# One more product of the identity ahead of the waits of o, h2 and yT in a two-layer transformer block kernel

## The chip, the cores and the metric

The kernel runs on one core of one Trainium2 chip. Times are microseconds on the device of one launch, from few repeated runs of the same program; the profiled execution is a run of its own.

## The reference

Sixteen sequences of 128 tokens with 128 features pass through two layers, each with self-attention, cross-attention to a context of 120 tokens, and an MLP:

```python
# layer 0, of x (16, 128, 128), context (16, 120, 128), condition c (16, 128); 16 heads of 8
shift_a, scale_a, gate_a, shift_m, scale_m, gate_m = split(silu(c) @ W_mod + b_mod, 6)
x = x + gate_a * (attention(modulate(ln(x), shift_a, scale_a)) @ W_proj + b_proj)
x = x + (cross_attention(ln(x), ln(context)) @ W_cproj + b_cproj)
h = gelu(modulate(ln(x), shift_m, scale_m) @ W_mlp1 + b_mlp1)
x = x + gate_m * (h @ W_mlp2 + b_mlp2)
# layer 1: the same three units with rotary positions, norms modulated by the condition, and no gates
x = x + attention(adaln(x)) @ sa_out_w.T
x = x + cross_attention(adaln(x), context) @ ca_out_w.T
x = x + (gelu(adaln(x) @ ffn_w1.T + ffn_b1) @ ffn_w2.T + ffn_b2)
```

## The kernel before, in words

The sixteen sequences are four streams of four (CB = 4, 512 columns). An attention unit f is one stream in one of four attention stages a (self and cross of layer 0, self and cross of layer 1), so there are 16 of them; the MLP units m are eight. Units are cut into steps, and make_plan() sorts all steps by times written out by hand in the table T. TensorE, SyncE and GpSimd go through the plan in that order, VectorE and ScalarE in the order of a second key (late). The order does not depend on what is ready: every engine works its list in turn, and semaphores hold it at a step whose data or buffer is missing.

The spine of the plan is the attention: a step "score" (L956) makes the scores of four heads into ps_sc, ScalarE takes their exponentials in two ACTIVATEs (L844), and "value" (L973) multiplies them with the values. The next score waits until both exponentials of the one before are done. All the rest stands between scores: norm transposes (xT, L879), projections (L918, L925), products for the row maxima (L936) with VectorE's reductions (L684) and their transpose (L942), transposes of the normalised sums (L982), the attention's output and the MLP.

Apart from ps_sc and ps_ao, all products go into five PSUM banks in turn (ps_misc, BANKS = 5). fill(n) waits until the reader of the use five before has finished. Then the step waits for its data. The steps that the change touches, all on TensorE:

- o (L992), only in the first self-attention stage, which has a gate: four times. It waits for attT, which ScalarE writes (L855). VectorE multiplies the result with the gate (yT_sb, L715).
- h2 (L1005), the second MLP product of layer 0: four times, four matmuls each. It waits for the four GELUs of ScalarE (hT, L861), which follow the four products of the first matrix (L999).
- yT (L1026), four transposes of yT_sb; behind o and behind h2, so eight times. It waits for VectorE's yT_sb; VectorE then adds the result to x (L728), whose statistics (L579, L582) and the root on GpSimd (L748) lead to the next normalised xn (L589).
- xT (L879), four transposes of xn, 24 times. It has two products ahead of its wait (warm, L875): the identity with the 384 columns of the constants, into the bank that the transposes then overwrite. Their result is read by nobody.

The other units end in a step "out" (L1019), which has no yT.

Of the kernel before, what the change touches and what calls it, by code (L numbers as in the profile page):

```python
# [61 lines left out]
PAIR = 2 * VW  # L62
VSLOTS = 3
PSLOTS = 4
WARM = 2


WCOLS = {}
# [27 lines left out]
NCONST = 3 * P  # L96
# [18 lines left out]
class Step:  # L115
# [34 lines left out]
    xT=(-32.06, -29.2, -31.0, -33.04),  # L150
# [184 lines left out]
def block_kernel(nc, weights, biases, consts, x_in, ctx_in, ctxT_in, rows_in, q_mem, k_mem, m_mem, out):  # L335
    plan, late, uses = make_plan()

    with ExitStack() as ctx:
# [88 lines left out]
        def bank(n):  # L427
            return ps_misc[:, n % BANKS, :]
# [62 lines left out]
        with nc.Block() as block:  # L491
# [374 lines left out]
            def _(pe):  # L866
                def fill(n):

                    if n >= BANKS:
                        pe.wait_ge(S[uses[n - BANKS][0]], uses[n - BANKS][1])  # L870

                def warm(use):

                    for _ in range(WARM):
                        pe.matmul(bank(use)[:, 0:NCONST], ident, cst[:, :], start=True, stop=True)  # L875

                def turn(src, use, rows=P):
                    for b in range(CB):
# [11 lines left out]
                for st in plan:  # L890
                    if st.kind == "xT":
                        fill(st.use)
                        warm(st.use)
                        pe.wait_ge(S["xn_ready"], CB * (st.k + 1))
                        turn(xn, st.use)
                    elif st.kind == "cT":
# [31 lines left out]
                    elif st.kind == "max":  # L928
                        ns = ns_of(st)
                        if st.b == 0:  # L930
                            pe.wait_ge(S["kd_ready"], HG * (st.f + 1))
                            pe.wait_ge(S["q_high"], st.f + 1)
                        for n in range(NG):
                            rows = slice(ROWS * n, ROWS * n + ROWS)
                            fill(st.use + n)
                            pe.matmul(bank(st.use + n)[:, 0:HG * ns], Qh[rows, st.f % 2, st.b * P:(st.b + 1) * P],  # L936
                                      Kd[rows, st.f % 2, :, st.b * ns:(st.b + 1) * ns],
                                      start=True, stop=True).then_inc(S["misc_filled"], 1)
                    elif st.kind == "mT":
                        fill(st.use)  # L940
                        pe.wait_ge(S["max_taken"], GROUPS * (st.f + 1))
                        pe.transpose(bank(st.use)[0:CB * H, 0:P], maxima[:, :, :].rearrange("p h b -> p (h b)"),  # L942
                                     ident).then_inc(S["misc_filled"], 1)
                    elif st.kind == "score":
                        ns = ns_of(st)
                        if st.b == 0 and st.g == 0:
                            pe.wait_ge(S[f"keys_in{st.f % 2}"], 16 * HG * (st.f // 2 + 1))
                            pe.wait_ge(S[f"queries_in{st.f % 2}"], 16 * HG * (st.f // 2 + 1))
                            pe.wait_ge(S[f"maxima_in{st.f % 2}"], 16 * HG * (st.f // 2 + 1))
                        if st.k:  # L950
                            pe.wait_ge(S["probs_ready"], GP * st.k)
                        for i in range(GP):
                            n = GP * st.g + i
                            for side in range(GP):
                                rows = slice(2 * TROWS * side, 2 * TROWS * side + TROWS + SR + 1)
                                ins = pe.matmul(ps_sc[0:ns, side, i * E * P:(i + 1) * E * P],  # L956
                                                Ks[rows, st.f % 2, n, st.b * ns:(st.b + 1) * ns],
                                                Qd[rows, st.f % 2, n, :, st.b * P:(st.b + 1) * P],
                                                start=True, stop=True)
                                if i == GP - 1:  # L960
                                    ins.then_inc(S[f"scores_ready{side}"], 1)
                    elif st.kind == "value":
                        ns = ns_of(st)
                        pe.wait_ge(S["probs_ready"], GP * (st.k + 1))
                        if st.b == 0 and st.g == 0:
                            pe.wait_ge(S["v_ready"], st.f + 1)
                        if st.k % CB == 0 and st.k:
                            pe.wait_ge(S["sums_copied"], st.k // CB)
                        heads = V[0:ns, st.f % VSLOTS, st.b, :, :].rearrange("p h r -> p (h r)")
                        for odd in range(2):  # L970
                            for c in range(HG):
                                at = PAIR * (HG * (GP * st.g + odd) + c) - VW * odd
                                last = pe.matmul(ps_ao[32 * c:32 * c + PAIR, st.b * P:(st.b + 1) * P],  # L973
                                                 heads[:, at:at + PAIR],
                                                 PT[0:ns, st.k % PSLOTS, c // E, odd, c % E, :],
                                                 start=not odd, stop=bool(odd))
                        last.then_inc(S["values_done"], 1)
                    elif st.kind == "norm":
                        fill(st.use)
                        pe.wait_ge(S["sums_copied"], st.k + 1)  # L980
                        for b in range(CB):
                            last = pe.transpose(bank(st.use)[:, b * P:(b + 1) * P],  # L982
                                                AOs[:, st.k % 2, b * P:(b + 1) * P], ident)
                        last.then_inc(S["misc_filled"], 1)
                    elif st.kind == "aT":
                        fill(st.use)
                        pe.wait_ge(S["att_ready"], CB * (st.f + 1))
                        turn(att, st.use)
                    elif st.kind == "o":
                        fill(st.use)  # L990
                        pe.wait_ge(S["attT_ready"], st.f + 1)
                        pe.matmul(bank(st.use), w(f"o{st.a}"), attT[:, :], start=True,  # L992
                                  stop=True).then_inc(S["misc_filled"], 1)
                    elif st.kind == "h":
                        fill(st.use)
                        pe.wait_ge(S["xnT_ready"], CB * (feeds["mlp", st.m] + 1))
                        if st.k == 0:
                            pe.wait_ge(S["rest_in"], 16)
                        pe.matmul(bank(st.use), w(f"w1_{st.a}", st.j), xnT[:, feeds["mlp", st.m] % 2, :],  # L999
                                  start=True, stop=True).then_inc(S["misc_filled"], 1)  # L1000
                    elif st.kind == "h2":
                        fill(st.use)
                        pe.wait_ge(S["hT_ready"], FF * (st.m + 1))
                        for j in range(FF):
                            last = pe.matmul(bank(st.use), w(f"w2_{st.a}", j), hT[:, j, :], start=(j == 0),  # L1005
                                             stop=(j == FF - 1))
                        last.then_inc(S["misc_filled"], 1)
                    elif st.kind == "out":

                        fill(st.use)  # L1010
                        if st.m is None:
                            pe.wait_ge(S["attT_ready"], st.f + 1)
                            parts = [(attT[:, :], w(f"o{st.a}"))]
                        else:
                            pe.wait_ge(S["hT_ready"], FF * (st.m + 1))
                            parts = [(hT[:, j, :], w(f"w2_{st.a}", j)) for j in range(FF)]
                        for b in range(CB):
                            for i, (src, weight) in enumerate(parts):
                                last = pe.matmul(bank(st.use)[:, b * D:(b + 1) * D], src[:, b * P:(b + 1) * P],  # L1019
                                                 weight, start=(i == 0), stop=(i == len(parts) - 1))  # L1020
                        last.then_inc(S["misc_filled"], 1)
                    elif st.kind == "yT":
                        fill(st.use)
                        pe.wait_ge(S["y_ready"], st.k + 1)
                        for b in range(CB):
                            last = pe.transpose(bank(st.use)[:, b * P:(b + 1) * P], yT_sb[:, b * P:(b + 1) * P],  # L1026
                                                ident)
                        last.then_inc(S["misc_filled"], 1)
# [71 lines left out]
```

## Time and profile before

| | us |
|---|---|
| median of 3 runs | 487.15 |
| lowest and highest | 484.03, 489.1 |
| profiled execution | 482.83 |
| its span, first to last instruction | 481.0 |
| mean granted TensorE clock of that span | 0.950 of full speed |

A row of the timeline is a group of instructions of one line that follow each other: its start in us from the span's start, its length, engine, line, operation and operands, how many, and in brackets how long the engine had been idle before it and who ended that. A float32 matmul that is no transpose shows two records. A row of the chain shows its start, its share on the chain and whose it is.

### The profile page before, as it was taken

The page shows a single profiled execution, that of the slowest core. Times are in us where ns is not written, and L with a number is a line of the kernel's source. Part 1 is how long each engine was busy: PE and PEld are TensorE (multiplying, and loading weights), DVE is VectorE, ACT ScalarE, POOL GpSimd, SP SyncE. Part 2 cuts the span into 40 slices and gives each one's busy share as a digit, 9 for nine tenths or more (in the row PEclk, how much of TensorE's full clock was granted, in tenths as well). Part 3 has the DMA queues.
Part 4 walks back from the last instruction along what each step waited for, and adds up shares of the span by engine and source line. Part 5 has one row for each costly group of instructions (what it writes and reads, how often), then busy time and mean ns, then how long its engine had stood idle before and what let it go on. Part 6 is the DMA issues. An engine that isn't in the chain of part 4 may idle for free.

```text
span 481.0 us, 10127 instructions
## 1 busy us (share of the span) xinstructions
PE 402.3 (84%) x3840; PEld 247.6 (51%) x3840; DVE 329.8 (69%) x841; ACT 267.8 (56%) x503; POOL 158.9 (33%) x138
## 2 busy tenths in 40 slices
PE   1855778899889979879888978989899998989696
PEld 1522444565565544544544534555565664747464
DVE  2666567899898963982974946878898994731331
ACT  1111265657666656465476556556565667576552
POOL 5762351651735520250241321335160542020130
PEclk9965699999999999998999989989999998999899
DMA  8860728285845631611613522545557472330001
GB/s 255 287 197 0 216 59 244 51 248 144 239 136 139 198 69 68 128 71 67 133 69 100 104 94 79 131 136 142 155 135 175 150 182 94 86 70 23 3 0 46
DMA packets 31272, 59.22 MB, mean 123 GB/s; under 512 B 3455, under 2 KB 7807, under 8 KB 30975
## 3 DMA queue, kind: packets, MB, share of 16 engines
q1 hardware_dynamic: 30935, 58.35, 44.1%
q8 instruction: 31, 0.51, 0.4%
q10 hardware_dynamic: 288, 0.21, 0.1%
q14 instruction: 18, 0.15, 0.1%
HBM read 31.81 MB, written 26.74 MB: 122 GB/s over the span
## 4 chain that ended last, share of the span: by engine, by line
PE 53%; DVE 16%; ACT 12%; POOL 10%; issue 5%; DMA 2%; SPq 1%; ACTq 0%; DVEq 0%; POOLq 0%
PE ps_ao L973 9%; POOL Kd L764 8%; PE ps_misc L999 7%; PE ps_sc L956 7%; DVE maxima L684 6%; PE ps_misc L875 6%; ACT PT L844 6%; PE ps_misc L918 5%; PE ps_misc L1019 4%; PE ps_misc L936 4%; PE ps_misc L879 4%; ACT xnT L830 3%; DVE xn L589 3%; PE ps_misc L1005 3%; POOL rstd L748 2%
## 5 line engine op out<-in xcount | busy, mean ns | idle before, releaser
L844 ACT ACTIVATE PT<-ps_sc 128x512 f32<-128x512 f32 (+1 forms) x256 | 138.9, 596 | 78.2 <-PE ps_sc L956 77.4
L684 DVE TENSOR_REDUCE maxima<-ps_misc 128x4 f32<-128x512 f32 (+1 forms) x256 | 154.1, 665 | 38.1 <-PE ps_misc L936 37.9
L764 POOL TENSOR_SCALAR Kd<-Kh,head_rows 128x512 fp32r<-128x512 f32 (+1 forms) x64 | 98.5, 1556 | 111.9 <-ACT Kh L804 82.4
L956 PE MATMUL ps_sc<-Qd,Ks 57*128 57x256 f32 (+1 forms) x512 | 64.6, 330 | 17.2 <-ACT PT L844 14.2
L973 PE MATMUL ps_ao<-PT,V 120*18 120x128 f32 (+1 forms) x2048 | 70.6, 277 | 2.8 <-ACT PT L844 2.7
L745 POOL TENSOR_SCALAR vareps<-mv 128x4 f32<-128x4 f32 (+1 forms) x28 | 6.8, 242 | 189.1 <-DVE mv L582 188.6
L956 PEld LDWEIGHTS ps_sc<-Qd,Ks 57*128 57x128 f32 (+1 forms) x512 | 37.7, 183 | 52.7 <-ACT PT L844 27.8
L830 ACT ACTIVATE xnT<-ps_misc,vec 128x128 f32<-128x128 f32 x80 | 30.1, 456 | 56.3 <-PE ps_misc L879 44.6
L973 PEld LDWEIGHTS ps_ao<-PT,V 120*18 120x18 f32 (+1 forms) x2048 | 50.3, 98 | 19.5 <-issue 8.1
L936 PE MATMUL ps_misc<-Kd,Qh 32*128 32x512 f32 (+1 forms) x256 | 42.2, 512 | 10.6 <-POOL Kd L764 8.8
L589 DVE TENSOR_SCALAR xn<-x,mv,rstd 128x128 f32<-128x128 f32 x96 | 36.5, 522 | 11.6 <-POOL rstd L748 11.6
L918 PE MATMUL ps_misc<-xnT,W 128*128 128x512 f32 x72 | 38.7, 653 | 6.8 <-ACT xnT L830 6.3
L875 PE MATMUL ps_misc<-cst 128*128 128x384 f32 x96 | 41.6, 562 | 1.5 <-DVE att L698 1.5
L728 DVE TENSOR_TENSOR x<-ps_misc,x 128x512 f32<-128x512 f32 x24 | 16.5, 687 | 36.9 <-PE ps_misc L1019 33.6
L999 PE MATMUL ps_misc<-xnT,W 128*128 128x512 f32 x64 | 34.3, 686 | 5.7 <-ACT xnT L830 5.0
L936 PEld LDWEIGHTS ps_misc<-Kd,Qh 32*128 32x128 f32 x256 | 17.5, 191 | 27.9 <-POOL Kd L764 9.3
L748 POOL TENSOR_TENSOR rstd<-vareps,minus_half 128x4 f32<-128x4 f32 (+1 forms) x28 | 29.3, 1047 | 2.3
L861 ACT ACTIVATE hT<-ps_misc,bias 128x512 f32<-128x512 f32 x32 | 21.7, 687 | 10.4 <-PE ps_misc L999 9.9
L715 DVE TENSOR_SCALAR yT_sb<-ps_misc,bias,vec 128x128 f32<-128x128 f32 x32 | 10.9, 403 | 23.3 <-PE ps_misc L1005 23.3
L875 PEld LDWEIGHTS ps_misc<-cst 128*128 128x128 f32 x96 | 18.5, 213 | 12.4 <-issue 3.3
L999 PEld LDWEIGHTS ps_misc<-xnT,W 128*128 128x128 f32 x64 | 13.3, 218 | 22.0 <-issue 15.9
L982 PE MATMUL ps_misc<-cst,AOs 128*128 128x128 f32 x128 | 20.2, 280 | 4.3 <-ACT AOs L850 3.3
(77 smaller groups left out, 471.2 us busy)
## 6 DMA issues: line engine op xcount, KB each, us to landing
Qd<-q_mem SPq DMA_DIRECT2D x64, 192.0 KB
k_mem<-Kh SPq DMA_DIRECT2D x16, 512.0 KB, 3.4
q_mem<-Qh SPq DMA_DIRECT2D x16, 512.0 KB, 2.9
Ks<-k_mem SPq DMA_DIRECT2D x32, 192.0 KB
Ks<-k_mem SPq DMA_DIRECT2D x32, 180.0 KB
k_mem<-Kl SPq DMA_DIRECT2D x16, 256.0 KB, 4.0
q_mem<-Ql SPq DMA_DIRECT2D x16, 256.0 KB, 3.0
W<-weights SPq DMA_DIRECT2D x1, 1792.0 KB, 18.5
```

The costliest lines, as they stand in the source:

```text
L589: dve.tensor_scalar(dst[0:rows, b, :], src[0:rows, b, :], mv[0:rows, which, b, 0:1], rstd[0:rows, which, b:b + 1], ALU.subtract, ALU.mult) ...
L684: dve.tensor_reduce(maxima[:, HG * n:HG * n + HG, st.b], bank(st.use + n)[:, 0:HG * ns].rearrange("p (h k) -> p h k", h=HG), AX_X, ALU.max ...
L748: pool.tensor_tensor(rstd[0:rows, which, :], vareps[0:rows, which, :], minus_half[0:rows, :], ALU.pow).then_inc(S["rstd_ready"], 1)
L764: pool.tensor_scalar(Kd[:, st.f % 2, c, 0:n], f32(Kh[:, st.f % 2, 0:n]), head_rows[:, c:c + 1], None, ALU.mult).then_inc(S["kd_ready"], 1)
L830: act.activation(dst[:, b * P:(b + 1) * P], src[:, b * P:(b + 1) * P], ACT.Identity, scale=vec[:, c, m:m + 1], bias=vec[:, c, sh:sh + 1]). ...
L844: act.activation(PT[0:ns, st.k % PSLOTS, g, :, :, :].rearrange("p i e t -> p (i e t)"), ps_sc[0:ns, g, :], ACT.Exp, scale=SCALE).then_inc( ...
L875: pe.matmul(bank(use)[:, 0:NCONST], ident, cst[:, :], start=True, stop=True)
L918: pe.matmul(bank(st.use + i)[:, 0:n], w(f"{st.kind}{st.a}{form}"), src[:, 0:n], start=True, stop=True).then_inc(S["misc_filled"], 1)
L936: pe.matmul(bank(st.use + n)[:, 0:HG * ns], Qh[rows, st.f % 2, st.b * P:(st.b + 1) * P], Kd[rows, st.f % 2, :, st.b * ns:(st.b + 1) * ns], ...
L956: ins = pe.matmul(ps_sc[0:ns, side, i * E * P:(i + 1) * E * P], Ks[rows, st.f % 2, n, st.b * ns:(st.b + 1) * ns], Qd[rows, st.f % 2, n, :, ...
L973: last = pe.matmul(ps_ao[32 * c:32 * c + PAIR, st.b * P:(st.b + 1) * P], heads[:, at:at + PAIR], PT[0:ns, st.k % PSLOTS, c // E, odd, c % ...
L999: pe.matmul(bank(st.use), w(f"w1_{st.a}", st.j), xnT[:, feeds["mlp", st.m] % 2, :], start=True, stop=True).then_inc(S["misc_filled"], 1)
```

## The change

The constant WARM becomes a table by kind of step. xT keeps its two products; o, h2 and yT have one each, placed between the wait for the bank and the wait for the data, into the bank that the step then writes.

```diff
-WARM = 2
+WARM = {"xT": 2, "o": 1, "h2": 1, "yT": 1}
...
-                def warm(use):
-
-                    for _ in range(WARM):
-                        pe.matmul(bank(use)[:, 0:NCONST], ident, cst[:, :], start=True, stop=True)
+                def warm(st):
+
+                    for _ in range(WARM[st.kind]):
+                        pe.matmul(bank(st.use)[:, 0:NCONST], ident, cst[:, :], start=True, stop=True)
...
                     if st.kind == "xT":
                         fill(st.use)
-                        warm(st.use)
+                        warm(st)
                         pe.wait_ge(S["xn_ready"], CB * (st.k + 1))
...
                     elif st.kind == "o":
                         fill(st.use)
+                        warm(st)
                         pe.wait_ge(S["attT_ready"], st.f + 1)
...
                     elif st.kind == "h2":
                         fill(st.use)
+                        warm(st)
                         pe.wait_ge(S["hT_ready"], FF * (st.m + 1))
...
                     elif st.kind == "yT":
                         fill(st.use)
+                        warm(st)
                         pe.wait_ge(S["y_ready"], st.k + 1)
```

## Rows read from the trace of the kernel before

**Rows 1.** The page: busy times of the engines; TensorE's granted clock in 40 slices.
```profile
PE 402.3 (84%) x3840; PEld 247.6 (51%) x3840; DVE 329.8 (69%) x841; ACT 267.8 (56%) x503; POOL 158.9 (33%) x138
...
PEclk9965699999999999998999989989999998999899
```

**Rows 2.** The page: the chain that ended last, shares by engine.
```profile
PE 53%; DVE 16%; ACT 12%; POOL 10%; issue 5%; DMA 2%; SPq 1%; ACTq 0%; DVEq 0%; POOLq 0%
```

**Rows 3.** Windows: stretch, length, busy PE, PEld, DVE, ACT, POOL, clock, DMA share, GB/s.
```profile
85.00:160.00 75.00, 67.96 (x802) 43.73 (x802) 69.41 (x197) 48.94 (x92) 35.42 (x32) 1.00 0.57 153
160.00:300.00 140.00, 120.06 (x1034) 68.38 (x1031) 94.16 (x242) 83.52 (x151) 38.40 (x36) 0.98 0.37 100
```

**Rows 4.** L875: the page's group, four timeline rows of TensorE, one of the chain.
```profile
L875 PE MATMUL ps_misc<-cst 128*128 128x384 f32 x96 | 41.6, 562 | 1.5 <-DVE att L698 1.5
...
104.34 1.56 PE L875 MATMUL ps_misc<-cst 128*128 128x384 f32 x4
105.73 0.60 PE L879 MATMUL ps_misc<-cst,xn 128*128 128x128 f32 x4
...
176.75 1.46 PE L875 MATMUL ps_misc<-cst 128*128 128x384 f32 x4
178.04 0.60 PE L879 MATMUL ps_misc<-cst,xn 128*128 128x128 f32 x4
...
36.59 2.86 PE ps_misc L875 x4
```

**Rows 5.** Timeline of TensorE around the first and the second o.
```profile
89.64 1.12 PE L992 MATMUL ps_misc<-attT,W 128*128 128x512 f32 x2
91.55 0.27 PE L942 MATMUL ps_misc<-cst,maxima 128*64 128x128 f32 x1 [0.79 <-DVE maxima L684]
...
109.44 0.51 PE L956 MATMUL ps_sc<-Qd,Ks 57*128 57x256 f32 x4 [0.18 <-ACT PT L844]
110.10 1.10 PE L992 MATMUL ps_misc<-attT,W 128*128 128x512 f32 x2 [0.16 <-ACT attT L855]
```

**Rows 6.** Timeline of TensorE (PEld: its weight load) around the second and fourth yT of the attention.
```profile
114.84 0.50 PE L956 MATMUL ps_sc<-Qd,Ks 57*128 57x256 f32 x4 [0.62 <-ACT PT L844]
115.27 0.66 PE L1026 MATMUL ps_misc<-cst,yT_sb 128*128 128x128 f32 x4
116.30 1.07 PE L973 MATMUL ps_ao<-PT,V 128*18 128x128 f32 x32
...
156.19 0.42 PEld L1026 LDWEIGHTS ps_misc<-cst,yT_sb 128*128 128x128 f32 x4 [0.29 <-DVE att L698]
156.77 1.21 PE L973 MATMUL ps_ao<-PT,V 120*18 120x128 f32 x32
```

**Rows 7.** Timeline of TensorE around the second h2 and its yT, and the fourth h2.
```profile
220.06 0.49 PE L956 MATMUL ps_sc<-Qd,Ks 57*120 57x256 f32 x4
221.00 3.67 PE L1005 MATMUL ps_misc<-hT,W 128*128 128x512 f32 x8 [0.45 <-ACT hT L861]
...
225.60 0.49 PE L956 MATMUL ps_sc<-Qd,Ks 57*120 57x256 f32 x4
226.23 0.63 PE L1026 MATMUL ps_misc<-cst,yT_sb 128*128 128x128 f32 x4
...
290.08 3.67 PE L1005 MATMUL ps_misc<-hT,W 128*128 128x512 f32 x8
```

**Rows 8.** Timeline of TensorE: xT waits and the first MLP product (L999) behind them.
```profile
212.42 0.66 PE L879 MATMUL ps_misc<-cst,xn 128*128 128x128 f32 x4 [1.06 <-DVE xn L589]
214.76 5.37 PE L999 MATMUL ps_misc<-xnT,W 128*128 128x512 f32 x8 [0.46 <-ACT xnT L830]
...
250.20 3.67 PE L999 MATMUL ps_misc<-xnT,W 128*128 128x512 f32 x8 [0.46 <-ACT xnT L830]
...
281.60 0.66 PE L879 MATMUL ps_misc<-cst,xn 128*128 128x128 f32 x4 [1.59 <-DVE xn L589]
283.95 5.26 PE L999 MATMUL ps_misc<-xnT,W 128*128 128x512 f32 x8 [1.25 <-ACT xnT L830]
```

## The prediction

> **What bounds the kernel now.** I read the page first: TensorE is busy 84% of the span, VectorE 69%, and the granted clock stands at nearly full speed but for the opening and five later slices that show an 8 [rows 1]. The chain that ended last lies 53% on TensorE, 16% on VectorE, 12% on ScalarE [rows 2]. So the program is bound by TensorE's in-order stream. Next come the stretches in which the new products stand: in 85 to 160 us the clock was 1.00 throughout, TensorE busy 67.96 of 75 us; in 160 to 300 us it was 0.98, busy 120.06 of 140 us [rows 3]. Last I read the timeline of TensorE around each of the 16 steps that the change touches. A product placed there is free only if TensorE would have waited at that very place, since what lies behind it on the engine is work that everything else follows. The length of a record includes the time until its result lands, so free time is read from starts: four score products take 0.43 us from their start to the next product's (114.84 to 115.27), though the record says 0.50 [rows 6].
>
> **What is added.** Nothing is removed or moved. xT keeps two products. o and h2 occur four times each (only the first layer's gated units have them), yT eight times, so 16 products of 128x384 in float32. The trace shows two records for one product (96 for 24 xT steps with two each) [rows 4]. Four records take from start to next start 178.04 - 176.75 = 1.29 us behind transposes, and 105.73 - 104.34 = 1.39 us behind scores [rows 4], so one product is 0.65 to 0.70 us of TensorE at the 2.4 GHz level; at 1.2 GHz four records were 2.86 us, one product 1.43 us [rows 4]. The stretches in question ran at the high level nearly throughout, so I use 0.65 to 0.70. Each stands behind the wait for the bank and ahead of the wait for the data; no semaphore, no DMA and no instruction of another engine is added.
>
> **o, four steps.** At 89.64 the product comes with no idle time before it, but then TensorE idles 0.79 us for VectorE's maxima before 91.55 [rows 5]. The added product goes into that idle time: 0. At 110.10 the scores had started at 109.44, TensorE was free at 109.87 and waited for attT: 0.23 us of cover [rows 5]. Left over: 0.42 to 0.47 us. Two more steps (130.45, 150.78) repeat the pattern. Behind them follow the queries' product, values and the next scores with no idle time, and the exponentials start from those scores, so it is all on the chain. Sum 1.26 to 1.41 us.
>
> **yT of the attention units, four steps.** At 115.27 they start 0.43 us behind the scores' start: no idle time at all, the data had long been ready [rows 6]. Three steps are like this (94.92, 115.27, 135.61): full price. The fourth (156.19) waits for its bank, not for its data (its weight load was released by VectorE's att, the bank's reader), and the product stands behind that wait, so full price too; but the values behind it (156.77) took 1.21 us instead of 1.07, being held within by ScalarE for some 0.14 us, which is cover [rows 6]. Sum 4 x 0.65 - 0.14 = 2.46 to 2.66 us.
>
> **h2, four steps.** At 221.00 the scores had started at 220.06, TensorE was free at 220.49: 0.51 us of real cover, the wait for the last GELU [rows 7]. Left over 0.14 to 0.19, three times (184.83, 221.00, 254.74). At 290.08 it came with no idle time, straight from transposes [rows 7], so 0.65 in full. Sum 1.07 to 1.22 us.
>
> **yT of the MLP units, four steps.** At 226.23 the scores had started at 225.60, so 0.20 us of cover [rows 7]; the others (190.05, 259.97, 295.31) have the same. Left over 0.45 to 0.50, sum 1.80 to 2.00 us. The transposes behind them feed the maxima products and the next scores, and at 295.31 the update of x and its statistics, which the chain runs through.
>
> Together 6.59 to 7.29 us; I take the middle, 6.9. If the covers of o and h2 and yT were gone the sum would be 16 x 0.70 = 11.2 us. From below: if the chain ran beside TensorE at the steps with some cover, only the four attention yT and the last h2 would count, some 3.1 us (2.46 + 0.65).
>
> **The clock.** This is the term that can be negative. The eight feed-forward records of one MLP lasted 3.67 us at 250.20, but 5.37 at 214.76 and 5.26 at 283.95, where the granted clock fell to the 1.2 GHz level [rows 8]: a fall costs 1.6 to 1.7 us. Ahead of the first, TensorE had stood idle 1.06 us for xn, ahead of the second 1.59 us, in xT steps that have two products already. None of the 16 places is there: the new products stand behind scores, between stretches of dense work, where the clock was at 2.4 GHz. So I count no gain. But everything from 90 us on comes later by another amount, and where falls happen may shift; I count that as zero in the mean and as 1 to 3 falls in the range.
>
> Rows 4 say that a pass of 384 columns takes 0.32 to 0.35 us. The Trainium skill (TensorE: Matmul & The Clock Gate, section Back-to-back issue gap) gives N/2.4 + 2.5 ns for a product, some 0.16 us a pass, an estimate by which a product in two passes is 0.33 us. With it the same sum would be 0.3 + 1.2 + 0.3 + 0.5 = 2.3 us. The trace does not agree, and its own duration is used.
>
> **The sum.** The profiled execution took 482.83 us (span 481.0, 1.8 us around it). With 6.9 it is 489.7. The median of the three runs is 487.15, 4.3 above the profiled one; the added work does not depend on that, so 487.15 + 6.9 = 494.0 (1.4% slower).
>
> **The rivals.** (A) The clock gives part back: the products keep TensorE busy enough that one to three of the five falls vanish. For it: idle time stood ahead of both falls of rows 8, and the median run lies 4.3 us above the profiled one, which has room for two more falls. Against: no new product lies in an xT wait. Each fall is 1.7 us, so with two 6.9 - 3.4 = +3.5: 490.7.
> (B) A product is worth only one of its records, for the other overlaps with what follows: by half the price of rows 4 (0.33) and the same covers +2.3 us, 489.4. Against it stand rows 4, where neither record overlapped. The Trainium skill's page cited above would give this result.
> (C) Not slower: all falls go. From the fifth fall on it decides, as 6.9 / 1.7 = 4.1. All five: 6.9 - 8.5 = -1.6, 485.5. If the falls that the other runs may have beyond the profiled one (4.3 us) go as well, it is -5.9, 481.2, faster by over 1%. For it speaks only that xT's products exist at all; against, that three of the five falls lie behind 300 us, where nothing is added [rows 1].
> (D) The covers don't hold, because what follows a late step is late in its turn (maxima, VectorE's updates, the xn waits lengthened, a fall more): 11.2 to 14 us, about 499.
> That the change does not what it says (a product while waiting) is in the forecast: at most places there is hardly any wait.
>
> **How the numbers follow.** Forecast (+5 to +9) 0.59; A 0.26; B 0.03; C 0.06; D 0.06. A measurement tells this kernel from no change at about 1%, here 4.9 us. Slower by over 1%: the forecast nearly whole and D, 0.61. Within: A, B, half of C and the forecast's edge, 0.34. Faster by over 1%: part of C and of luck in the clock, 0.05. The range takes in A from its middle and the forecast, and half of D: 488.0 to 498.5.
>
> **What would show it.** The product's group has 128 records instead of 96, at 486 ns where the clock is high, and TensorE's busy time is up by some 10 us. Scores behind o at 110 us come 0.45 later, those behind each attention yT 0.65 to 0.70 later; by 160 us the program is some 4 us late, by 300 us about 7. At the first o the idle time before the maxima's transpose is down from 0.79 to about 0.1. At h2 the wait for the GELU has gone. The five falls stay five, give or take two. I am wrong if the shift by 160 us is under 2 us (then the chain did not run through TensorE), or if the shift is there and is given back later, by fewer falls.

## The result and the profile after

The changed kernel is slower: ratio 1.0117, 95% interval 1.0088 to 1.0146, from 22 executions of each. The medians are 483.14 us before and 489.12 after. The three runs shown ahead of the prediction had a median of 487.15, 4 us above that of the 22, so the forecast's 494.0 carries that with it; the forecast difference was +6.9 us, the measured one 483.14 x 0.0117 = +5.7 (6.0 between the medians). The profiled execution of the changed kernel took 486.92 us. Here and below a ratio leaves out executions over 1.5% above the fastest of the same kernel (seven of twelve in e2, three of seven in e7b), and the other columns of the table of experiments use all but two executions.

The page of the changed kernel, answering to [rows 1, 2]:

```profile
span 485.1 us, 10175 instructions
...
PE 410.0 (85%) x3872; PEld 253.6 (52%) x3872; DVE 329.7 (68%) x841; ACT 267.7 (55%) x503; POOL 159.1 (33%) x138
...
PEclk9966688999999999999998999989999999999999
...
PE 54%; DVE 16%; ACT 11%; POOL 9%; issue 5%; DMA 2%; SPq 1%; ACTq 0%; DVEq 0%; POOLq 0%
...
L875 PE MATMUL ps_misc<-cst 128*128 128x384 f32 x128 | 56.2, 555 | 1.8 <-DVE att L698 1.5
```

There are 32 more matmul records, TensorE is 7.7 us longer busy, and the other engines have what they had. The clock row shows two 8s behind the opening (the first seven slices, here 9966688) instead of five; a third fall of the clock, at about 459 us, lies across two slices (four products' records that begin at 459.19 take 2.56 us instead of 1.46).

The second o and the yT behind it, in TensorE's timeline of the changed kernel, to be read beside [rows 5, 6]; then the product's weight loads (PEld) and ScalarE's attT at the same place:

```profile
109.85 0.50 PE L956 MATMUL ps_sc<-Qd,Ks 57*128 57x256 f32 x4 [0.21 <-ACT PT L844]
110.43 0.91 PE L875 MATMUL ps_misc<-cst 128*128 128x384 f32 x2
111.18 1.02 PE L993 MATMUL ps_misc<-attT,W 128*128 128x512 f32 x2
...
115.83 0.50 PE L956 MATMUL ps_sc<-Qd,Ks 57*128 57x256 f32 x4 [0.65 <-ACT PT L844]
116.26 0.91 PE L875 MATMUL ps_misc<-cst 128*128 128x384 f32 x2
117.01 0.60 PE L1029 MATMUL ps_misc<-cst,yT_sb 128*128 128x128 f32 x4
117.45 0.60 PE L982 MATMUL ps_misc<-cst,AOs 128*128 128x128 f32 x4
```
```profile
110.43 0.30 PEld L875 LDWEIGHTS ps_misc<-cst 128*128 128x128 f32 x2 [0.28 <-ACT attT L855]
...
109.69 0.69 ACT L855 ACTIVATE attT<-ps_misc,bias 128x512 f32<-128x512 f32 x1
```

At yT the product runs straight behind the scores, 0.75 us from its start to yT's; as the transposes themselves now take 0.44 instead of 0.50 to the next line's start, the step is 0.69 longer in all. At o something else is to be seen. TensorE is free at 110.28, yet the product starts at 110.43 only: its weight load was released by attT (109.69 + 0.69 = 110.38), though the product stands ahead of the wait for attT. The plan says why. The bank of the second, third and fourth o is the one that aT used five products before, and a bank that aT used is free once attT_ready has reached this very number. The wait for the bank and the wait for the data are the same wait, and the product stands behind it.

The second h2 and its yT, and the third MLP, to be read beside [rows 7, 8]:

```profile
217.19 0.65 PE L879 MATMUL ps_misc<-cst,xn 128*128 128x128 f32 x4 [1.06 <-DVE xn L589]
...
219.53 3.67 PE L1000 MATMUL ps_misc<-xnT,W 128*128 128x512 f32 x8 [0.46 <-ACT xnT L830]
223.14 0.50 PE L956 MATMUL ps_sc<-Qd,Ks 57*120 57x256 f32 x4
223.56 0.91 PE L875 MATMUL ps_misc<-cst 128*128 128x384 f32 x2
224.31 3.60 PE L1007 MATMUL ps_misc<-hT,W 128*128 128x512 f32 x8
...
253.96 5.37 PE L1000 MATMUL ps_misc<-xnT,W 128*128 128x512 f32 x8 [0.46 <-ACT xnT L830]
```

From the scores to h2 it is 224.31 - 223.14 = 1.17 us, before 0.94: 0.23 late. The same MLP product that took 5.37 us before takes 3.67 here behind the same 1.06 us of idle time, and the next unit's takes 5.37 where it took 3.67. So these two falls of the clock moved from one unit to another; no product stands between xT and the MLP product in either kernel.

Following the same instruction through both traces (start after less start before) gives the shift at every step. A price in the table is the shift at a step's own start less that at the step of the table before it, with the falls of the clock taken out (the first yT's 0.70 has already what comes back right behind it). The changed kernel was 0.28 us early when it came to the first o.

| | shift added, us | forecast |
|---|---|---|
| first o | 0 (the maxima's transpose stays at -0.28) | 0 |
| second to fourth o | 0.66, 0.60, 0.60 = 1.86 | 1.26 to 1.41 |
| four yT of the attention | 0.70, 0.66, 0.68, 0.67, less 0.19 given back = 2.52 | 2.46 to 2.66 |
| four h2 | 0.22, 0.24, 0.24, 0.64 = 1.34 | 1.07 to 1.22 |
| four yT of the MLP, with what is given back behind them | 0.45, 0.44, 0.45, 0.45 = 1.79 | 1.80 to 2.00 |
| sum | 7.5 | 6.6 to 7.3 |

The spans differ by 4.1 us only: -0.28 + 7.5, and the 3.1 us that are missing go with falls of the clock, of which this execution had two fewer behind 85 us.

### The profile page after: what moved, and what is told of

It reads as the page before. It is cut to its first block, busy times and chain, and to the rows that moved or that the text cites. A ratio compares the mean times of both kernels' runs of the same rounds, so it can differ in the third digit from the quotient of the medians.

```text
span 485.1 us, 10175 instructions
## 1 busy us (share of the span) xinstructions
PE 410.0 (85%) x3872; PEld 253.6 (52%) x3872; DVE 329.7 (68%) x841; ACT 267.7 (55%) x503; POOL 159.1 (33%) x138
## 4 chain that ended last, share of the span: by engine, by line
PE 54%; DVE 16%; ACT 11%; POOL 9%; issue 5%; DMA 2%; SPq 1%; ACTq 0%; DVEq 0%; POOLq 0%
PE ps_ao L973 9%; PE ps_misc L875 8%; POOL Kd L764 7%; PE ps_sc L956 7%; PE ps_misc L1000 6%; DVE maxima L684 6%; ACT PT L844 5%; PE ps_misc L918 4%; PE ps_misc L1021 4%; PE ps_misc L936 4%; PE ps_misc L879 4%; ACT xnT L830 3%; DVE xn L589 3%; PE ps_misc L1007 3%; PE ps_misc L982 2%
## 5 line engine op out<-in xcount | busy, mean ns | idle before, releaser
L875 PE MATMUL ps_misc<-cst 128*128 128x384 f32 x128 | 56.2, 555 | 1.8 <-DVE att L698 1.5
L589 DVE TENSOR_SCALAR xn<-x,mv,rstd 128x128 f32<-128x128 f32 x96 | 35.0, 505 | 11.6 <-POOL rstd L748 11.6
L918 PE MATMUL ps_misc<-xnT,W 128*128 128x512 f32 x72 | 37.1, 629 | 6.7 <-ACT xnT L830 6.2
L1000 PE MATMUL ps_misc<-xnT,W 128*128 128x512 f32 x64 | 31.0, 630 | 5.6 <-ACT xnT L830 4.9
L875 PEld LDWEIGHTS ps_misc<-cst 128*128 128x128 f32 x128 | 23.0, 204 | 15.0 <-issue 3.5
L692 DVE RECIPROCAL rden<-ps_misc 128x32 f32<-128x32 f32 x32 | 11.2, 352 | 18.5 <-PE ps_misc L982 18.4
```

What stands on the lines that cost most here:

```text
L589: dve.tensor_scalar(dst[0:rows, b, :], src[0:rows, b, :], mv[0:rows, which, b, 0:1], rstd[0:rows, which, b:b + 1], ALU.subtract, ALU.mult) ...
L875: pe.matmul(bank(st.use)[:, 0:NCONST], ident, cst[:, :], start=True, stop=True)
L918: pe.matmul(bank(st.use + i)[:, 0:n], w(f"{st.kind}{st.a}{form}"), src[:, 0:n], start=True, stop=True).then_inc(S["misc_filled"], 1)
```

## The experiments

Each time comes with the mean granted clock of its execution. The time at the lower level is 2 x (1 - clock) x span: 48 us in the profiled execution before. Over 204 executions, the changed kernel's 22 among them, a line through the times of each kernel against this number, with one slope for all, has slope 0.33 and leaves 1.1 us unexplained (the standard deviation about the lines): one microsecond at the lower level goes with 0.33 us of time. The distance between two such lines is the difference at equal clock, free of most of the scatter. The Trainium skill (TensorE: Matmul & The Clock Gate, section Terms) puts the penalty at throttled time x (1 - K/N), K/N being the granted share of the clock, by which an estimate for the lower level, half of the upper, is 0.5. The runs show 0.33, as a mean over places that need not be alike: of the 48 us of the profiled execution before, 31 lie in the first 85 us, where no product is added. The first 85 us of e5 do the same work as those of the kernel before, at a clock of 0.73 instead of 0.82, which is 15 us more at the lower level, and e5 comes out of them 5.2 us later: 0.33 per us again. TensorE is busy for only 55 of these 85 us, which may be why; it wasn't tried. The windows from 0 to 85 us of the kernel before and of e5, columns as in [rows 3]:

```profile
0.00:85.00 85.00, 55.01 (x332) 31.75 (x332) 49.87 (x119) 25.39 (x52) 37.94 (x30) 0.82 0.60 179
...
0.00:85.00 85.00, 55.69 (x278) 32.00 (x282) 47.27 (x114) 21.56 (x43) 37.98 (x30) 0.73 0.60 178
```

| | ratio, interval | at equal clock, us | us at the lower level |
|---|---|---|---|
| before (73 executions) | 1 | 0 | 48.7 ± 1.0 |
| changed (22) | 1.0117, 1.0088 to 1.0146 | +7.1 ± 0.3 | 45.3 ± 1.3 |
| e1 only o | 1.003, 0.9984 to 1.0075 | +1.4 ± 0.4 | 51.8 ± 2.9 |
| e2 only yT | 1.0011, 0.9955 to 1.0067 | +3.7 ± 0.4 | 44.6 ± 2.1 |
| e3 only h2 | 0.9978, 0.9933 to 1.0023 | +0.5 ± 0.4 | 45.0 ± 2.3 |
| e4 o's product behind the wait | 1.0112, 1.0056 to 1.0168 | +7.3 ± 0.5 | 40.6 ± 2.9 |
| e5 two products each | 1.0424, 1.0351 to 1.0497 | +17.6 ± 0.5 | 55.1 ± 2.2 |
| e6 128 columns | 1.0041, 0.9987 to 1.0095 | +2.1 ± 0.4 | 48.4 ± 2.3 |
| e7 xT one, none elsewhere | 0.9865, 0.9777 to 0.9953 | -9.4 ± 0.5 | 59.4 ± 3.3 |
| e7b the same | 0.9794, 0.9728 to 0.986 | -8.9 ± 0.4 | 56.7 ± 2.6 |
| e8 xT one, o, h2, yT one | 1.0037, 0.9998 to 1.0076 | -2.2 ± 0.4 | 59.6 ± 1.4 |
| e9 no product at all | 1.0051, 1.0007 to 1.0094 | -15.0 ± 0.4 | 100.4 ± 1.6 |
| e10 xT one, MLP one | 0.9928, 0.989 to 0.9965 | -6.4 ± 0.4 | 56.7 ± 1.7 |

The ± are standard errors. The changed kernel's executions and those of the kernel before in this table come from different sessions, and e7b to e10 ran on another chip than e1 to e7; with the clock's part taken out, the kernel before itself differs by at most 0.6 us between its three sessions. Its own time at the lower level in them was 46.7 ± 1.5 (e1 to e4), 51.8 ± 2.7 (e5 to e7) and 49.1 ± 1.6 us (e7b to e10).

**The parts alone.** Three kernels that keep only one kind of product.

```diff
-WARM = {"xT": 2, "o": 1, "h2": 1, "yT": 1}
+WARM = {"xT": 2, "o": 1, "h2": 0, "yT": 0}   # e1
+WARM = {"xT": 2, "o": 0, "h2": 0, "yT": 1}   # e2
+WARM = {"xT": 2, "o": 0, "h2": 1, "yT": 0}   # e3
```

> Only the four products ahead of o; none at h2 and yT. Theory (price 0.65 to 0.70 us, no cover at the second to fourth o because the bank's wait and the data's wait are for the same attT): the steps behind the second, third and fourth o start 0.60 to 0.66 us later each in the trace, the first o costs 0; together +1.9 us, ratio 1.004. Rival (0.23 us of cover as forecast): 0.42 to 0.47 each, +1.3 us. Rival clock (a good part of the cost of the whole change is offset because the products keep the clock up): one fall fewer than before, ratio under 1.002.

> Only the eight products ahead of yT. Theory: +0.66 to 0.70 us at each of the four attention yT, less 0.2 to 0.3 behind the fourth, and +0.45 to 0.50 at each MLP yT: +4.3 us of displacement, ratio 1.009. Rival clock: the displacement is there in the trace, but the granted clock of the runs is higher than that of the kernel before and the ratio is 1.005 or less.

> Only the four products ahead of h2. Theory: +0.22 us three times and +0.64 at the fourth, +1.3 us, ratio 1.003. Rival (h2's product is free, the GELU's wait covers it): +0.6 us or less. Rival clock: the falls ahead of the MLP go, ratio 0.997 or less.

In the traces the shifts stand at the expected places. e1: 0 at the first o, then 0.66, 0.57, 0.59. e2: 0.69, 0.74, 0.69, 0.70 at the yT of the attention units, and 0.52 to 0.55 at those of the MLP. e3: 0.21, 0.23, 0.17 and 0.63. With what is given back, and without the falls, the three traces are shifted by 1.8, 4.7 and 1.0 us in all, which is the 7.5 of the whole. So o's cover of 0.23 us is refuted and h2's of 0.51 confirmed. The ratios say little: none of the three differs from 1, and those of e2 and e3 lie below the 1.009 and 1.003 expected, e2's by more than its interval. The means of all twelve executions of each stand at 1.0066, 1.0064 and 1.0001 of that of the kernel before in the same session. At equal clock they are +1.4, +3.7 and +0.5, together 5.6 where the whole has 7.1 and the traces 7.5; the order is that of the traces, the sum is short, and why is not shown. On the clock rival they can't decide: e2's ratio is what that rival asked for, but 51.8, 44.6 and 45.0 us at the lower level lie about the 46.7 of the kernel before in their session.

**The same wait twice.** If the bank's wait is the data's wait at o, moving the product behind both changes nothing.

```diff
                         fill(st.use)
-                        warm(st)
                         pe.wait_ge(S["attT_ready"], st.f + 1)
+                        warm(st)
```

> The changed kernel whole, but the product of o stands behind the wait for attT instead of ahead of it. Theory (bank and data wait are for the same semaphore value at the second to fourth o, so the product ran behind it anyway): the distance from the scores' start to o's start stays 1.33 us, and the time is that of the changed kernel, ratio to before 1.012. Rival (the product used the idle time ahead of o): the distance grows by 0.2 us, 0.6 us in all.

> The product of o behind the wait for attT once more, for a trace of an undisturbed execution. Theory: scores' start to o's start 1.33 us at the second to fourth o, as in the changed kernel. Rival: 1.5 us or more.

The ratio is 1.0112 beside 1.0117; the profiled execution of e4 was one of the two that are left out, hence e4b. The third o in the trace of e4b (the first fence) and in that of the changed kernel (the second):

```profile
129.99 0.50 PE L956 MATMUL ps_sc<-Qd,Ks 57*128 57x256 f32 x4 [0.23 <-ACT PT L844]
130.66 0.88 PE L875 MATMUL ps_misc<-cst 128*128 128x384 f32 x2 [0.17 <-ACT attT L855]
131.38 1.02 PE L993 MATMUL ps_misc<-attT,W 128*128 128x512 f32 x2
```
```profile
131.47 0.50 PE L956 MATMUL ps_sc<-Qd,Ks 57*128 57x256 f32 x4 [0.23 <-ACT PT L844]
132.04 0.91 PE L875 MATMUL ps_misc<-cst 128*128 128x384 f32 x2
132.79 1.02 PE L993 MATMUL ps_misc<-attT,W 128*128 128x512 f32 x2
```

It is 1.39 us from the scores to o against 1.32 in the changed kernel, at all three o alike to 0.01, nearer to the theory's 1.33 than to 1.5. The place ahead of the wait was worth 0.07 us of the 0.23 that TensorE was idle.

**Twice, and a third of the columns.**

```diff
+WARM = {"xT": 2, "o": 2, "h2": 2, "yT": 2}   # e5
...
+                        n = NCONST if st.kind == "xT" else P   # e6, with one product each
+                        pe.matmul(bank(st.use)[:, 0:n], ident, cst[:, 0:n], start=True, stop=True)
```

> Two products instead of one ahead of o, h2 and yT (xT keeps two). Theory (in-order displacement, all cover is used up by the first product): the second costs 0.65 us at fifteen places and about 0.55 at the first o, so +10.3 us over the changed kernel, +17.6 over the kernel before at equal clock, ratio 1.035. Rival clock (products buy clock): the time at the 1.2 GHz level falls by 10 us or more against the changed kernel and the ratio is under 1.028.

> The changed kernel with the added products cut to 128 of the 384 columns. Theory (price goes with the columns, 0.22 us a product): 0.2 each at three o, four attention yT and the last h2, nothing at the first o and at the first three h2, at most 0.05 at the MLP yT: +1.8 us at equal clock, ratio 1.004. Rival (a fixed price per product, its weight load and the change of data type): 0.4 us or more each, +4.5 us.

e5 came out at +17.6 us at equal clock, exactly the sum. Its four records at the second o (116.84 to 118.24) take 1.40 us, 0.65 more than two:

```profile
116.84 1.56 PE L875 MATMUL ps_misc<-cst 128*128 128x384 f32 x4
118.24 1.02 PE L993 MATMUL ps_misc<-attT,W 128*128 128x512 f32 x2
```

Its time at the lower level is not 10 us shorter than the changed kernel's but 10 longer, so the clock rival is refuted for these places, where a product stands between dense work. The ratio, 1.0424, is above the expected 1.035, in part by that: 3 to 6 us more at the lower level than before are 1 to 2 us.

e6, TensorE's timeline around the same two places as above:

```profile
110.00 0.50 PE L957 MATMUL ps_sc<-Qd,Ks 57*128 57x256 f32 x4 [0.21 <-ACT PT L844]
110.58 0.49 PE L876 MATMUL ps_misc<-cst 128*128 128x128 f32 x2
110.90 1.02 PE L994 MATMUL ps_misc<-attT,W 128*128 128x512 f32 x2
...
115.99 0.49 PE L876 MATMUL ps_misc<-cst 128*128 128x128 f32 x2
116.31 0.60 PE L1030 MATMUL ps_misc<-cst,yT_sb 128*128 128x128 f32 x4
```

A product of 128 columns holds up the step behind it by 0.32 us, one of 384 for 0.75: 0.43 for 256 columns in two records, and about 0.1 that doesn't depend on the columns. The +2.1 us agree with the theory's 1.8 and not with the fixed price.

**Fewer products at xT.** So products cost their length. Do they ever buy clock?

```diff
+WARM = {"xT": 1, "o": 0, "h2": 0, "yT": 0}   # e7, e7b
+WARM = {"xT": 1, "o": 1, "h2": 1, "yT": 1}   # e8
+WARM = {"xT": 0, "o": 0, "h2": 0, "yT": 0}   # e9
```

> The kernel before with one product ahead of xT instead of two, none elsewhere. Theory (a product costs 0.65 us wherever TensorE doesn't wait behind it, and buys clock only where it fills a real wait): at about 18 of 24 xT steps 0.65 us goes, some 8 to 11 us at equal clock, and the time at the 1.2 GHz level grows by 5 us or more, which gives 2 us or more back. Rival clock: the time at the lower level grows so much that the ratio is 1.00 or above. Rival none (no clock effect at all): the time at the lower level stays within 3 us and the ratio is 0.98.

> The kernel before with one product ahead of xT, once more beside the next three. From the first time: 9 us less at equal clock, some 10 us more at the 1.2 GHz level, ratio 0.984 to 0.988.

> One product ahead of xT, and one each ahead of o, h2 and yT. Theory (the costs add, and the added products buy no clock): +7.2 us against the run with xT's one product alone, at equal clock, and the same time at the 1.2 GHz level within 3 us; ratio to before 0.998 to 1.002. Rival (with the clock weaker, the added products keep it up): the time at the lower level falls by 6 us or more and the ratio is 0.993 or less.

> No product of the identity anywhere. Theory (xT's first product mostly stood in real waits): only at about half of the 24 steps does it free 0.65 us, so 5 to 9 us less at equal clock than with one product, and 10 us or more at the 1.2 GHz level come on top, which give back 3 us or more; ratio 0.970 to 0.985. Rival clock: the clock stays low for long stretches, ratio above 0.99.

e7 and e7b: 9 us less at equal clock, 8 to 11 us more at the lower level, and faster than the kernel before, by 1.4% and 2.1%. e7b's ratio is below the expected 0.984 to 0.988. The mean of all 13 executions of the two, 476.6, against 482.7 of the kernel before is 1.3% less, which I take as the better number. The rival without any clock effect asked for a time at the lower level within 3 us of before, and is out. Where the second product had hidden a wait, the wait is now on the page (TensorE's waits, e7; before it was 4.7 us in 6 times):

```profile
PE ps_misc L879 <- DVE xn L589: 12.8, 11, 2.3
```

e8 is 7.0 us above e7 and e7b at equal clock (-2.2 against -9.1), as the costs add, and its time at the lower level is 59.6 us, that of e7: with a weaker clock too, the products at o, h2 and yT bought nothing that shows. The rival asked for 6 us less. The ratio, 1.0037, is above the 0.998 to 1.002 expected, which its interval reaches.

e9 is the other side. At equal clock it is 15 us faster than before, and it throws all of it away: 100 us at the lower level, twice as much, cost 0.33 x 52 = 17 us. Both are read with the slope, but the trace has the same: the xT that [rows 4] show at 178.04 starts at 167.30, 10.7 us early, and at 300 us e9 is only 1.4 us early. The ratio, 1.0051, is outside what the theory gave (0.970 to 0.985), though its 5 to 9 us at equal clock beside e7 were right (5.9): the clock rival was right for the first product at xT. Windows of e9 by stretch, columns as in [rows 3], and e9's wait for xn and one of its xT:

```profile
85.00:160.00 75.00, 65.10 (x817) 42.50 (x817) 72.65 (x202) 51.10 (x97) 38.38 (x36) 1.00 0.66 182
160.00:300.00 140.00, 114.92 (x930) 63.20 (x928) 87.95 (x226) 77.94 (x139) 31.55 (x30) 0.87 0.32 86
300.00:482.00 182.00, 157.05 (x1642) 102.28 (x1642) 115.31 (x281) 110.03 (x210) 46.73 (x40) 0.92 0.37 100
```
```profile
PE ps_misc L879 <- DVE xn L589: 22.4, 13, 3.0
...
167.30 0.60 PE L879 MATMUL ps_misc<-cst,xn 128*128 128x128 f32 x4
```

Between 160 and 300 us the clock is 0.87 where it was 0.98 before. Six of e9's thirteen waits for xn end in that stretch, of 1.2 to 3.0 us each; it has layer 0's MLP units and the first rotary projections. Between 85 and 160 us it stays at 1.00 without any product.

**A product in another real wait.** The first MLP product waits for xnT in six units (5.0 us in all, up to 1.25); a product there should be nearly free.

```diff
                     elif st.kind == "h":
                         fill(st.use)
+                        if st.j == 0:
+                            warm(st)
                         pe.wait_ge(S["xnT_ready"], CB * (feeds["mlp", st.m] + 1))
```

> One product ahead of xT and one ahead of the first MLP product of each of the eight MLP units (behind its bank's wait, ahead of the wait for xnT), none at o, h2 and yT. Theory (there TensorE really waits, 0.4 to 1.2 us, so the product is mostly cover): at most 2 us more at equal clock than with xT's one product alone. If products buy clock where they fill a real wait ahead of dense work, the time at the 1.2 GHz level falls by 5 us or more; if not it stays within 3 us.

At equal clock it costs 2.8 us beside e7 and e7b (-6.4 against -9.1), more than the 2 expected, and the time at the lower level stays at 56.7 us. Its timeline shows why:

```profile
211.22 0.91 PE L875 MATMUL ps_misc<-cst 128*128 128x384 f32 x2 [0.37 <-ACT xnT L830]
211.97 2.31 PE L1002 MATMUL ps_misc<-xnT,W 128*128 128x512 f32 x5
```

The product was itself released by xnT. In the four MLP units of layer 0 the first MLP product takes the bank that xT used five products before, and that bank's wait is for the same count of xnT_ready as the data's: o's case again, and I had walked into it a second time. Compared with e7, the added product delays the MLP's own by 0.69, 0.64 and 0.63 us at the first three of these units. In the last two units of layer 1, where TensorE does not wait for xnT, it delays it by 0.5 and 0.6 us as well. These are most of the 2.8 us. So this run doesn't tell whether a product that fills this wait would buy clock; that stays open. It is faster than the kernel before (0.9928), through xT, and slower than e7.

## Why the prediction was right

**What bounds the kernel**: right. The chain runs through TensorE's order of work, and nearly all that was added shows up as a shift that is never given back.

**The price of a product** (0.65 to 0.70 us): right; 0.64 to 0.70 in the table at every place without cover, and 17.6 us at equal clock for 32 products, as summed up before the run.

**yT and h2**: right for yT, step by step, and a little low for h2 (1.34 against up to 1.22). The cover at h2, 0.51 us, was there; 0.22 to 0.24 were left over where 0.14 to 0.19 stood, as a product delays what follows it by up to 0.75, not 0.70, behind scores. The 0.14 given back behind the fourth yT was 0.19.

**o**: this term was mis-sized. "TensorE was free at 109.87 and waited for attT: 0.23 us of cover" took any idle time in front of the step as cover. But the product stands behind the wait for the bank, and at three of four o steps that is the same event as the data. It measured 1.86 us in place of 1.26 to 1.41 (1.74 if it is read behind o's second record, as some 0.07 of each comes back there). I had made this very distinction for the fourth yT and not for o. The first o, with the maxima's wait behind it, cost 0 as forecast.

**The sum**: 6.9 forecast, 7.5 in the trace, 7.1 ± 0.3 at equal clock. The time itself, 489.1, is nearer to A's 490.7 than to the forecast's 494.0, but that comes from the base of 487.15: put on 483.14, the forecast is 490.0 and A 486.6. That the range from 488.0 held in spite of this base is in part luck, as the result stands 1.1 us above its lower end.

**The clock** (counted as zero): nearly right. 7.1 at equal clock and 5.7 in the ratio leave 1.4 us, the size of one fall, in favour of the changed kernel; its time at the lower level is 3.4 ± 1.6 us shorter, and that of e4, with the same products, 8 ± 3. So a sign that the prediction had named for its being wrong, a shift that fewer falls give back later, did come, in part: 3.1 of 7.5 us in the profiled execution, some 1.4 us in the ratio. Rival A in its own size (one to three falls) is not excluded by that, but its reason has the experiments against it: e5 and e8 have the same products or more of them and spend no less time at the lower level. That the falls come at other places once everything is shifted is the simpler reading; that was not shown by itself, and stays open. B, half the price, is refuted by e5 and by the records. C and D did not come. The estimate from the Trainium skill (TensorE: Matmul & The Clock Gate, section Back-to-back issue gap) that would have given B, 0.16 us a pass, is half of what one record of 384 float32 columns took, 0.32 us.

**The profile's predictions**: 128 records, as said. By 160 us the shift was 4.4, by 300 us 7.5 less the falls. Busy time was up by 7.7, not 10 us, as fewer falls also make other products shorter. The five falls, which were to stay "five, give or take two", were three, at the edge of that.

## What to carry to other kernels

A dummy instruction put ahead of a wait fills only the idle time behind its own place: look which semaphore releases the instruction itself (here the buffer's, which at o and at the MLP's first product was the data's under another name), and whether the engine waits there at all. Where it doesn't, it costs its full length in an engine that bounds the kernel. And more of such clock-keeping products are not always better: here, by the slope of 0.33, the first at xT cost 6 us of work and gave back 14 us of clock (0.33 x 42), the second cost 9 and gave back 3, so that of none, one and two, one was the fastest.

## What was not expected of the hardware

One microsecond at the lower clock level goes with 0.33 us of this kernel's time, and the scatter between executions of one program (478 to 489 us) is nearly all clock: with it taken out 1.1 us are left. Where two versions of a kernel differ by less than the scatter, the clock of each execution told them apart where the times alone did not.

Two executions took about twice the usual time or more: the first of e4, 917.16 us, and one of the kernel before, 1175.94. In the trace of the first the granted clock is 1.00 throughout, the other engines' durations are the usual ones, and matmuls take more than twice as long (the projections 1413 ns, in the changed kernel 629). The cause is open; both are left out above.

```profile
L918 PE MATMUL ps_misc<-xnT,W 128*128 128x512 f32 x72 | 90.0, 1413 | 4.3 <-ACT xnT L830 4.3
```
